# Attention with a mixture of experts on one core: the PV group is issued between the score pair and the maximum passes instead of behind both

## The chip, the core and the metric

The kernel runs on one core of a Trainium2 chip. The number is device time in microseconds for one launch, the median of several runs. The engines here: TensorE (PE in the rows; its weight loads are listed apart, as PEld), VectorE (DVE), ScalarE (ACT), GpSimd (POOL) and SyncE (SP), which issues most transfers. Each runs its own instruction stream in order, and semaphores hold an instruction until others have finished.

## What is computed

One layer: cross attention with residual, then a feed-forward block with residual. B = 8, C = 256 channels, T = 512; 16 heads of 16 channels, attention over the 512 columns of the context.

```python
# attention: x is _layernorm(x), c is ctx_2048
q = jnp.einsum('oc,bct->bot', Wq, x) + bq[None, :, None]   # k, v alike from c
scores = jnp.einsum('bhkt,bhks->bhts', q, k) * SCALE
p = jax.nn.softmax(scores, axis=-1)
out = jnp.einsum('bhts,bhks->bhkt', p, v)
# ... output projection Wo, added to x
# feed-forward: router, softmax, top 2 of 8 experts, and a shared expert
moe = jnp.einsum('te,ted->td', w_dense, eo)
sh = jax.nn.silu(ht @ sw_gate) * (ht @ sw_up) @ sw_down
x = x + moe + sh
```

## The kernel before

The kernel has two stages. The attention stage comes first; the feed-forward stage (shared expert, routing, then 39 blocks of gathered rows) follows it. The change is in the attention stage alone.

The attention works through 16 halves (`HALVES`), each of 8 heads of one batch element; `s` numbers them. A half has 32 units (`UNITS`): one unit is a 128 x 512 tile of scores of one head. Two jobs run beside each other on TensorE:

- `scores(s, u)` (L646 to L660, matmul at L658) multiplies keys by queries, with the row maxima already folded into two extra rows of the operands, and ACT then takes the exponential of the tile (L555) into `probs`. It writes one of three banks of `st_ps` and waits until the exponential of three units before has emptied it.
- `max_pass(n, u)` (L616 to L627, matmul at L625) computes the same scores the other way round for a later half (one to two halves ahead), only so that DVE can take the row maxima (L751, `negmax`). It writes one of three banks of `smax_ps` and waits until the maximum of three passes before is taken (`pe.wait_ge(max_done, i - MAXBUF + 1)`).

`pv(k)` (L662 to L675, matmuls at L671) multiplies the probabilities of four units by the values. It needs the exponentials of all four (`pe.wait_ge(exp_done, GH * (k + 1))`), and is issued in the step after them. `project_qk`, `project_v`, `project_out` and `turn_max` are larger or single products for later or earlier halves: query and key projection (L597, u = 2 and 6, for half s + 3), value projection (L612) in even halves or output projection (L272) in odd halves from 3 on (u = 18 and 26; in half 0 u = 10 and 14), and the transposition of the maxima (L644, u = 12; in half 0 u = 16).

The loop over `u` in steps of two, in the function for TensorE (L704 to L728), is written out by hand and sets the order: two scores, then as many maximum passes as `maxima_until(s, u)` allows (four per pair early in half 0, then three, then two; none behind the last half), then the PV group if `u` is a multiple of 4, then the larger products. The DVE function walks through the same `maxima_until` table (L795 on), and adds behind the maxima: `max_parts` at u = 14, `residual` (L339) at u = 20 and 28 and its statistics (L793) at u = 22 and 30 in odd halves from 3 on, and a few steps of the layer norm in halves 1 to 3 and 14.

Of the kernel before, what the change touches and what calls it, by code (L numbers as in the profile page):

```python
# [21 lines left out]
GH = 4  # L22
UNITS = HH * TT
STEPS = UNITS // GH
# [25 lines left out]
def xattn_ffn_kernel(nc, x, ctxt, wqkv_t, wo_t, bias_cols, rms_w, router_t, gate_up, down,  # L50
# [16 lines left out]
    with ExitStack() as outer:  # L67
# [116 lines left out]
        def turn_unit(s):  # L184

            return 16 if s == 0 else 12

        def late_units(s):

            return (10, 14) if s == 0 else (18, 26)  # L190

        def value_batch(s):

            return s // 2 + 1 if s % 2 == 0 and s // 2 + 1 < B else None

        def maxima_until(s, u):

            pairs = u // TILES + 1
            if s == 0:
                ahead = min(UNITS + AHEAD + 4 * pairs, UNITS + AHEAD + 4 + 3 * pairs, UNITS + AHEAD + 12 + 2 * pairs)  # L200
            elif s < 3:
                ahead = min(80 + 36 * (s - 1) + 3 * pairs, 84 + 36 * (s - 1) + 2 * pairs)
            else:
                ahead = UNITS * (s + 2) - 8 + 2 * pairs
            return min(ahead, UNITS * HALVES)
# [19 lines left out]
        def out_batch(s):  # L225

            return (s - 3) // 2 if s % 2 == 1 and s >= 3 else None
# [4 lines left out]
        def score_bank(i):  # L232
            return st_ps[:, i % STBUF, :]
# [122 lines left out]
        with nc.Block() as block:  # L356
# [211 lines left out]
            def _(pe):  # L568
# [11 lines left out]
                def project_qk(n, i):  # L580
                    s = n - 3
                    if i == 0:
                        pe.wait_ge(c_loaded[(n // 2) % 2], 16 * (n // 4 + 1))
                        if n == 1:
                            pe.wait_ge(qk32_ready, 2)
                        if n == 2:
                            pe.wait_ge(vt_copied, 2)
                        if s >= 0:
                            pe.wait_ge(nm_parts_ready, turns(s))
                            pe.wait_ge(vt_copied, values_before(s))  # L590
                            pe.wait_ge(x1_ready, X1_START + CT * outputs_before(s))
                    else:
                        pe.wait_ge(qk32_ready, 2 * n + 1)
                        pe.wait_ge(xn_ready, n // 2 + 1)
                    src = c_sb[:, (n // 2) % 2, :, :] if i == 0 else xn
                    for kt in range(CT):
                        mm = nc.tensor.matmul(proj_ps[:, :], w_t[:, i, kt, (n % 2) * P:(n % 2) * P + P],  # L597
                                              src[:, kt, :], start=(kt == 0), stop=(kt == CT - 1))
                    mm.then_inc(qk_ready, 1)

                def project_v(b, r):

                    if r == 1:
                        pe.wait_ge(vt_copied, 2 * b + 1)
                    elif b < 2:
                        pe.wait_ge(qk32_ready, 4 * (b + 1))
                    else:
                        pe.wait_ge(nm_parts_ready, turns(2 * b - 1))
                    for i in range(2):
                        st = 2 * r + i  # L610
                        for kt in range(CT):
                            mm = nc.tensor.matmul(proj_ps[:, C * i:C * (i + 1)], c_sb[:, b % 2, kt, st * P:(st + 1) * P],  # L612
                                                  w_t[:, 2, kt, :], start=(kt == 0), stop=(kt == CT - 1))
                    mm.then_inc(v_ready, 1)

                def max_pass(n, u):  # L616
                    buf = n % NBUF
                    if u == 0:
                        pe.wait_ge(stack_loaded[buf], 16 * 2 * 2 * TILES * (n // NBUF + 1))
                    i = UNITS * n + u  # L620
                    if i >= MAXBUF:
                        pe.wait_ge(max_done, i - MAXBUF + 1)
                    tile, pair, tt = u % TILES, u // TILES // TT, u // TILES % TT
                    low = HALFP * tile
                    nc.tensor.matmul(smax_bank(i), q_stack[buf][low:low + SROWS, pair, tt * P:(tt + 1) * P],  # L625
                                     k_stack[buf][low:low + SROWS, pair, :], start=True, stop=True,
                                     tile_position=(low, 0)).then_inc(s_ready, 1)  # L627
# [11 lines left out]
                def turn_max(n):  # L639
                    pe.wait_ge(qk32_ready, 2 * min(n + 3, HALVES))  # L640
                    pe.wait_ge(vt_copied, values_before(max(n - 1, 1)))
                    pe.wait_ge(x1_ready, X1_START + CT * outputs_before(n - 1))
                    pe.wait_ge(max_done, UNITS * (n + 1))
                    nc.tensor.transpose(proj_ps[0:UNITS, 0:P], negmax[:, n % 2, :], ident[:, :]).then_inc(nm_turned, 1)  # L644

                def scores(s, u):  # L646
                    g, st, j = u // (GH * TT), u // GH % TT, u % GH
                    buf = s % NBUF
                    if s == 0 and u == 0:
                        pe.wait_ge(first_loaded, 16 * TILES)  # L650
                        pe.wait_ge(ones_loaded, 16 * TILES * NBUF)
                    if u == (HALF_UNITS if s == 0 else 0):
                        pe.wait_ge(rows_loaded[buf], 16 * TILES * (s // NBUF + 1))
                    i = UNITS * s + u
                    if i >= STBUF:
                        pe.wait_ge(exp_done, i - STBUF + 1)
                    low, pair, end = HALFP * (j % TILES), 2 * g + j // TILES, HALFP * (j % TILES) + SROWS + PARTS
                    nc.tensor.matmul(score_bank(i), k_stack[buf][low:end, pair, st * P:(st + 1) * P],  # L658
                                     q_stack[buf][low:end, pair, :], start=True, stop=True,
                                     tile_position=(low, 0)).then_inc(st_ready, 1)  # L660

                def pv(k):  # L662
                    n, g, st = k // STEPS, k // TT % 2, k % TT
                    pe.wait_ge(exp_done, GH * (k + 1))
                    if st == 0 and k >= TT:
                        pe.wait_ge(pv_copied, k // TT)
                    if st == 0 and g == 0:
                        pe.wait_ge(vt_copied, 2 * (n // 2 + 1))
                        pe.wait_ge(v_ones, min(n + 1, NBUF))
                    for j in range(GH):  # L670
                        mm = nc.tensor.matmul(pv_ps[32 * j:32 * j + 32, :], v_t[n % NBUF][:, st, GH * g + j, :],  # L671
                                              probs[:, k % 2, j, :], start=(st == 0), stop=(st == TT - 1),
                                              tile_position=(0, 32 * j))
                    mm.then_inc(pv_done, 1)
# [29 lines left out]
                for s in range(HALVES):  # L704
                    for u in range(0, UNITS, TILES):
                        scores(s, u)
                        scores(s, u + 1)
                        while passed < maxima_until(s, u):
                            max_pass(passed // UNITS, passed % UNITS)
                            passed += 1  # L710
                        if u % GH == 0 and STEPS * s + u // GH >= 1:
                            pv(STEPS * s + u // GH - 1)
                        if s + 3 < HALVES and u in KQ_UNITS:
                            project_qk(s + 3, KQ_UNITS.index(u))
                        if u == turn_unit(s) and s + 1 < HALVES:
                            turn_max(s + 1)
                        if value_batch(s) is not None and u in late_units(s):
                            project_v(value_batch(s), late_units(s).index(u))
                        if out_batch(s) is not None and u in late_units(s):
                            for kt in range(CT):  # L720
                                project_out(pe, out_batch(s), late_units(s).index(u), kt, proj_ps[:, :])
                        if s == HALVES - 2 and u == 12:
                            pe.wait_ge(max_done, UNITS * HALVES)
                        if UNITS * s + u > UNITS * (HALVES - 2) + 12 and u % GH == 2:
                            filler(smax_bank(0))
# [691 lines left out]
```

## Time and profile before

| what | value |
|---|---|
| median of 3 runs | 936.95 us (926.53 to 937.61) |
| the profiled execution | 931.33 us |
| its span (first to last instruction) | 929.5 us |
| PE busy | 863.4 us, 93% |
| DVE busy | 484.5 us, 52% |
| ACT busy | 400.0 us, 43% |
| maxima (L751 on DVE) | 512, 323.6 us |
| exponentials (L555 on ACT) | 512, 279.3 us |
| PV matmul rows (L671) | 1024 (8 for each of 128 groups), 138.9 us |
| score matmuls (L658), maximum passes (L625) | 512 each, 157.2 and 142.0 us |

Rows of the trace give the start of an instruction, or of a run of equal ones, in microseconds from the span's start, and how long it was busy. Matmuls are pipelined, so a start is a better mark than an end: two matmuls on different rows of the array overlap, and a row of two lasts hardly longer than one. A weight load (PEld) shows the wait of the matmul that it belongs to.

### The profile page before, as it was taken

Reading aid. Unit: us, or ns where it says so; the run is one execution under the profiler, and the core shown is the slowest. Engines: PE = TensorE matmul, PEld = TensorE weight load, DVE = VectorE, ACT = ScalarE, POOL = GpSimd, SP = SyncE. Lnnn points to the kernel's source line nnn. Section 1 sums busy time; section 2 is a strip of 40 time slices with the busy share of each in tenths; the row PEclk is TensorE's granted clock in tenths of the full one; section 3 lists DMA queues with packets and bytes.
Section 4 is the critical chain, followed back from the end, with each engine's and each line's share of the span. In section 5 each row is a group of like instructions: output and inputs, shape, how many; then the busy total and the mean of one; then the engine's idle time right before and its main releaser. Section 6 shows DMA issues by size and latency. Waiting matters only on the chain. (4 is left out here: it accounts for less than half of the span.)

```text
span 929.5 us, 10794 instructions
## 1 busy us (share of the span) xinstructions
PE 863.4 (93%) x3575; PEld 373.2 (40%) x3575; DVE 484.5 (52%) x978; ACT 400.0 (43%) x755; POOL 223.5 (24%) x206
## 2 busy tenths in 40 slices
PE   6699989999999999999999989969999999999992
PEld 2234334334333343333432345725444444444440
DVE  4486788777777777777786056491221111111110
ACT  1104666656666676676765741300012222222220
POOL 3113013213142131421100021000104444444441
PEclk9798999999999999999997989799999999999997
DMA  6877465645655566555611139400725555555542
GB/s 221 183 181 180 95 153 129 150 96 130 146 133 116 114 145 144 135 110 105 140 40 39 37 92 369 164 1 2 278 82 91 91 91 90 91 91 91 91 80 34
DMA packets 46872, 110.43 MB, mean 119 GB/s; under 512 B 11668, under 2 KB 12692, under 8 KB 42580
## 3 DMA queue, kind: packets, MB, share of 16 engines
q1 hardware_dynamic: 35404, 80.23, 34.6%
q0 software_dynamic: 11328, 29.37, 15.6%
q8 instruction: 30, 0.49, 0.2%
q14 instruction: 22, 0.18, 0.1%
q10 hardware_dynamic: 88, 0.16, 0.0%
HBM read 68.44 MB, written 41.16 MB: 118 GB/s over the span
## 5 line engine op out<-in xcount | busy, mean ns | idle before, releaser
L751 DVE TENSOR_REDUCE negmax<-smax_ps 128x1 f32<-128x512 f32 x512 | 323.6, 682 | 107.7 <-PE smax_ps L625 107.5
L555 ACT ACTIVATE probs<-st_ps 128x512 f32<-128x512 f32 x512 | 279.3, 600 | 188.4 <-PE st_ps L658 188.1
L658 PE MATMUL st_ps<-q_stack,k_stack 50*128 50x512 f32 x512 | 157.2, 495 | 10.6 <-ACT probs L555 8.2
L625 PE MATMUL smax_ps<-k_stack,q_stack 48*128 48x512 f32 x512 | 142.0, 438 | 13.5 <-DMA q_stack<-parts_dram 6.9
L1178 PE MATMUL big_ps<-w_gu,attn 128*128 x312 | 140.4, 593 | 0.8 <-ACT attn L1019 0.8
L671 PE MATMUL pv_ps<-probs,v_t 128*32 128x512 f32 x1024 | 138.9, 615 | 0.8 <-ACT probs L555 0.5
L658 PEld LDWEIGHTS st_ps<-q_stack,k_stack 50*128 50x128 f32 x512 | 60.1, 186 | 185.7 <-ACT probs L555 148.7
L985 POOL DMA_INDIRECT out<-x_sb,row_i x39 | 61.7, 1582 | 140.0 <-ACT x_sb L1026 130.2
L1364 DVE TENSOR_TENSOR zeros<-attn,big_ps 128x256 f32<-128x256 f32 x39 | 16.4, 422 | 135.0 <-ACT attn L1038 135.0
L625 PEld LDWEIGHTS smax_ps<-k_stack,q_stack 48*128 48x128 f32 x512 | 67.5, 188 | 46.5 <-DVE negmax L751 29.2
L1178 PEld LDWEIGHTS big_ps<-w_gu,attn 128*128 128x128 f32 x312 | 56.2, 190 | 57.0 <-issue 57.0
L1146 PE MATMUL big_ps<-rows_or_down,zeros 128*128 x156 | 73.5, 593 | 0.6 <-DVE zeros L1356 0.6
L334 POOL TENSOR_TENSOR attn<-attn,recip 128x512 f32<-128x512 f32 x15 | 19.2, 1280 | 223.7 <-DMA recip<-rec_dram 223.7
L1038 ACT ACTIVATE attn<-big_ps 128x256 f32<-128x256 f32 x39 | 15.0, 385 | 117.7 <-PE big_ps L1178 117.7
L1072 PE MATMUL big_ps<-ht_all,sh_gu 128*128 128x512 f32 x128 | 60.8, 632 | 0.7 <-DVE pv_raw L1205 0.7
L970 POOL DMA_INDIRECT x_sb<-h_rows,row_i x39 | 38.8, 995 | 91.9 <-DMA out<-x_sb 80.3
L458 POOL CAST parts<-qk 128x512 fp32r<-128x512 f32 x28 | 17.1, 612 | 173.7 <-ACT qk L508 171.0
L1356 DVE COPY zeros<-big_ps 128x256 f32<-128x256 f32 x39 | 16.6, 425 | 58.5 <-PE big_ps L1155 58.5
L1026 ACT ACTIVATE x_sb<-big_ps,weight 128x512 f32<-128x512 f32 x39 | 26.8, 687 | 45.0 <-PE big_ps L1146 34.9
L462 POOL TENSOR_TENSOR parts<-qk,parts 128x512 fp32r<-128x512 f32 x32 | 40.7, 1273 | 21.5 <-DVE parts L743 19.3
L1072 PEld LDWEIGHTS big_ps<-ht_all,sh_gu 128*128 128x128 f32 x128 | 25.7, 204 | 32.5 <-issue 32.5
L597 PE MATMUL proj_ps<-c_sb,w_t 128*128 128x512 f32 x64 | 36.7, 701 | 1.2 <-ACT qk L508 0.9
(156 smaller groups left out, 719.0 us busy)
## 6 DMA issues: line engine op xcount, KB each, us to landing
parts_dram<-parts SPq DMA_DIRECT2D x32, 512.0 KB, 6.1
k_stack<-parts_dram SPq DMA_DIRECT2D x32, 256.0 KB, 4.9
q_stack<-parts_dram SPq DMA_DIRECT2D x32, 256.0 KB, 5.6
w_gu<-in_gate_up SPq DMA_DIRECT2D x8, 1024.0 KB, 15.5
x_sb<-in_x SPq DMA_DIRECT2D x8, 512.0 KB, 8.1
c_sb<-in_ctx POOLq DMA_DIRECT2D x8, 512.0 KB, 7.9
k_stack<-parts_dram SPq DMA_DIRECT2D x32, 128.0 KB, 5.4
q_stack<-parts_dram SPq DMA_DIRECT2D x32, 128.0 KB, 6.1
```

What stands on the lines that cost most here:

```text
L462: nc.gpsimd.tensor_tensor(parts[:, i, 1, :], qk32[:, i, :], parts[:, i, 0, :].bitcast(F32), ALU.subtract).then_inc(low_ready, 1)
L555: nc.scalar.activation(probs[:, k % 2, u % GH, :], score_bank(UNITS * s + u), ACT.Exp, scale=SCALE).then_inc(exp_done, 1)
L597: mm = nc.tensor.matmul(proj_ps[:, :], w_t[:, i, kt, (n % 2) * P:(n % 2) * P + P], src[:, kt, :], start=(kt == 0), stop=(kt == CT - 1))
L625: nc.tensor.matmul(smax_bank(i), q_stack[buf][low:low + SROWS, pair, tt * P:(tt + 1) * P], k_stack[buf][low:low + SROWS, pair, :], start=T ...
L658: nc.tensor.matmul(score_bank(i), k_stack[buf][low:end, pair, st * P:(st + 1) * P], q_stack[buf][low:end, pair, :], start=True, stop=True, ...
L671: mm = nc.tensor.matmul(pv_ps[32 * j:32 * j + 32, :], v_t[n % NBUF][:, st, GH * g + j, :], probs[:, k % 2, j, :], start=(st == 0), stop=(s ...
L751: nc.vector.tensor_reduce(negmax[:, n % 2, c:c + 1], smax_bank(UNITS * n + u), AX_X, ALU.max, negate=True).then_inc(max_done, 1)
L970: nc.gpsimd.indirect_dma_start(h_in[:, k % RING, :], None, h_rows, bass.IndirectOffsetOnAxis(ap=row_i[:, k:k + 1], axis=0)).then_inc(in_lo ...
L985: nc.gpsimd.indirect_dma_start(out_rows, bass.IndirectOffsetOnAxis(ap=row_i[:, k:k + 1], axis=0), y_sb[:, k % RING, :], None, compute_op=A ...
L1072: mm = nc.tensor.matmul(big_ps[:, 2 * (j % 2) + i, :], sh_gu[:, a, i * F + c * P:i * F + (c + 1) * P], ht_all[:, g, a, :], start=(a == 0), ...
L1146: mm = nc.tensor.matmul(y_ps[:, k % 2, :], act_t[:, a, :], w_dn[:, bass.ds(expert, 1), a, :], start=(a == 0), stop=(a == FT - 1))
L1178: mm = nc.tensor.matmul(gu_ps[:, :], h_t[:, k % 2, a, :], w_gu[:, bass.ds(expert, 1), a, :], start=(a == 0), stop=(a == DT - 1))
```

## The change

The call of `pv` moves up by four lines: in the half-steps with `u` a multiple of 4 the PV group is now issued right behind the two scores and ahead of the maximum passes. Its waits and its operands are the same. No instruction is added or removed, and the order on DVE, ACT, POOL and SP is the same as before.

```diff
--- before.py
+++ after.py
@@ -705,11 +705,11 @@
                     for u in range(0, UNITS, TILES):
                         scores(s, u)
                         scores(s, u + 1)
+                        if u % GH == 0 and STEPS * s + u // GH >= 1:
+                            pv(STEPS * s + u // GH - 1)
                         while passed < maxima_until(s, u):
                             max_pass(passed // UNITS, passed % UNITS)
                             passed += 1
-                        if u % GH == 0 and STEPS * s + u // GH >= 1:
-                            pv(STEPS * s + u // GH - 1)
                         if s + 3 < HALVES and u in KQ_UNITS:
                             project_qk(s + 3, KQ_UNITS.index(u))
                         if u == turn_unit(s) and s + 1 < HALVES:
```

On TensorE, at the start of half 3 (u = 0 to 8), before. `st_ps` rows are score pairs, `smax_ps` rows maximum passes, `pv_ps` rows the PV group, `proj_ps` rows the key and query projections:

```order
L658 MATMUL st_ps<-q_stack3,k_stack3 128x512 x2
L625 MATMUL smax_ps<-k_stack0,q_stack0 128x512 x2
L671 MATMUL pv_ps<-probs,v_t2 32x512 x4
L658 MATMUL st_ps<-q_stack3,k_stack3 128x512 x2
L625 MATMUL smax_ps<-k_stack0,q_stack0 128x512 x2
L597 MATMUL proj_ps<-c_sb,w_t 128x512 x2
L658 MATMUL st_ps<-q_stack3,k_stack3 128x512 x2
L625 MATMUL smax_ps<-k_stack0,q_stack0 128x512 x2
L671 MATMUL pv_ps<-probs,v_t3 32x512 x4
L658 MATMUL st_ps<-q_stack3,k_stack3 128x512 x2
L625 MATMUL smax_ps<-k_stack0,q_stack0 128x512 x2
L597 MATMUL proj_ps<-xn,w_t 128x512 x2
L658 MATMUL st_ps<-q_stack3,k_stack3 128x512 x2
```

The same place in the changed kernel:

```order
L658 MATMUL st_ps<-q_stack3,k_stack3 128x512 x2
L671 MATMUL pv_ps<-probs,v_t2 32x512 x4
L625 MATMUL smax_ps<-k_stack0,q_stack0 128x512 x2
L658 MATMUL st_ps<-q_stack3,k_stack3 128x512 x2
L625 MATMUL smax_ps<-k_stack0,q_stack0 128x512 x2
L597 MATMUL proj_ps<-c_sb,w_t 128x512 x2
L658 MATMUL st_ps<-q_stack3,k_stack3 128x512 x2
L671 MATMUL pv_ps<-probs,v_t3 32x512 x4
L625 MATMUL smax_ps<-k_stack0,q_stack0 128x512 x2
L658 MATMUL st_ps<-q_stack3,k_stack3 128x512 x2
L625 MATMUL smax_ps<-k_stack0,q_stack0 128x512 x2
L597 MATMUL proj_ps<-xn,w_t 128x512 x2
L658 MATMUL st_ps<-q_stack3,k_stack3 128x512 x2
```

In each step the PV row has changed places with the passes in front of it. The passes of u = 0 (and 4) now stand one score pair ahead of the passes of u = 2 (and 6), with nothing else between; and between the passes of u = 2 and those of u = 4 there are the projection, the scores and the PV group.

On TensorE at the start of half 1, where three passes follow a pair, before and then changed:

```order
L658 MATMUL st_ps<-q_stack1,k_stack1 128x512 x2
L625 MATMUL smax_ps<-k_stack2,q_stack2 128x512 x3
L671 MATMUL pv_ps<-probs,v_t0 32x512 x4
L658 MATMUL st_ps<-q_stack1,k_stack1 128x512 x2
L625 MATMUL smax_ps<-k_stack2,q_stack2 128x512 x3
L597 MATMUL proj_ps<-c_sb,w_t 128x512 x2
L658 MATMUL st_ps<-q_stack1,k_stack1 128x512 x2
L625 MATMUL smax_ps<-k_stack2,q_stack2 128x512 x3
```

```order
L658 MATMUL st_ps<-q_stack1,k_stack1 128x512 x2
L671 MATMUL pv_ps<-probs,v_t0 32x512 x4
L625 MATMUL smax_ps<-k_stack2,q_stack2 128x512 x3
L658 MATMUL st_ps<-q_stack1,k_stack1 128x512 x2
L625 MATMUL smax_ps<-k_stack2,q_stack2 128x512 x3
L597 MATMUL proj_ps<-c_sb,w_t 128x512 x2
L658 MATMUL st_ps<-q_stack1,k_stack1 128x512 x2
L671 MATMUL pv_ps<-probs,v_t1 32x512 x4
```

Here six passes stand with only one score pair in the middle. In the last half, and in half 14 from u = 8 on, there are no passes, and the order is the same in both kernels.

## Rows read from the trace of the kernel before

**Rows 1.** Page, part 1: busy us (share of the span) x instructions.

```profile
PE 863.4 (93%) x3575; PEld 373.2 (40%) x3575; DVE 484.5 (52%) x978; ACT 400.0 (43%) x755; POOL 223.5 (24%) x206
```

**Rows 2.** Timeline of PE, half 4, u = 20 to 28: start, us, what.

```profile
217.21 0.50 PE L658 MATMUL st_ps<-q_stack,k_stack 50*128 50x512 f32 x2
217.55 0.40 PE L625 MATMUL smax_ps<-k_stack,q_stack 48*128 48x512 f32 x2
217.87 1.07 PE L671 MATMUL pv_ps<-probs,v_t 128*32 128x512 f32 x8
218.87 0.51 PE L658 MATMUL st_ps<-q_stack,k_stack 50*128 50x512 f32 x2
219.20 0.41 PE L625 MATMUL smax_ps<-k_stack,q_stack 48*128 48x512 f32 x2
219.44 1.10 PE L658 MATMUL st_ps<-q_stack,k_stack 50*128 50x512 f32 x2
220.05 0.82 PE L625 MATMUL smax_ps<-k_stack,q_stack 48*128 48x512 f32 x2
220.81 1.06 PE L671 MATMUL pv_ps<-probs,v_t 128*32 128x512 f32 x8
...
222.14 0.39 PE L625 MATMUL smax_ps<-k_stack,q_stack 48*128 48x512 f32 x2
222.46 1.99 PE L612 MATMUL proj_ps<-w_t,c_sb 128*128 128x256 f32 x8
224.38 0.50 PE L658 MATMUL st_ps<-q_stack,k_stack 50*128 50x512 f32 x2
```

**Rows 3.** Timeline of DVE, half 4, behind u = 26 and 30.

```profile
222.56 1.29 DVE L751 TENSOR_REDUCE negmax<-smax_ps 128x1 f32<-128x512 f32 x2 [0.44 <-PE smax_ps L625]
...
226.82 0.69 DVE L751 TENSOR_REDUCE negmax<-smax_ps 128x1 f32<-128x512 f32 x1 [0.38 <-PE smax_ps L625]
```

**Rows 4.** Timeline of all engines, half 7, around u = 24.

```profile
306.75 0.74 DVE L339 SCALAR_TENSOR_TENSOR x_sb<-proj_ps,bo_all,x_sb 128x512 f32<-128x512 f32 x1
...
307.41 1.28 DVE L751 TENSOR_REDUCE negmax<-smax_ps 128x1 f32<-128x512 f32 x2
...
307.62 0.50 PE L658 MATMUL st_ps<-q_stack,k_stack 50*128 50x512 f32 x1 [0.22 <-ACT probs L555]
...
308.14 0.18 PEld L625 LDWEIGHTS smax_ps<-k_stack,q_stack 48*128 48x128 f32 x1 [0.34 <-DVE negmax L751]
...
308.57 1.06 PE L671 MATMUL pv_ps<-probs,v_t 128*32 128x512 f32 x8
308.60 0.68 DVE L793 BATCH_NORM_STATS2 stats<-x_sb 128x6 f32<-128x512 f32 x1
309.20 2.46 DVE L751 TENSOR_REDUCE negmax<-smax_ps 128x1 f32<-128x512 f32 x4
...
312.27 0.50 PE L658 MATMUL st_ps<-q_stack,k_stack 50*128 50x512 f32 x2
```

**Rows 5.** Waits, 197.3 to 461.1 us: us in total, times, longest.

```profile
PEld smax_ps L625 <- DVE negmax L751: 4.4, 18, 0.3
```

**Rows 6.** Timeline of PE, half 15, u = 8.

```profile
524.73 0.50 PE L658 MATMUL st_ps<-q_stack,k_stack 50*128 50x512 f32 x2
525.16 1.06 PE L671 MATMUL pv_ps<-probs,v_t 128*32 128x512 f32 x8
```

**Rows 7.** Timeline of ACT, half 4, u = 26 and 27.

```profile
222.33 1.08 ACT L555 ACTIVATE probs<-st_ps 128x512 f32<-128x512 f32 x2 [0.87 <-PE st_ps L658]
```

**Rows 8.** Timeline of PE, half 2, u = 4 and 8.

```profile
141.19 0.50 PE L658 MATMUL st_ps<-q_stack,k_stack 50*128 50x512 f32 x2
...
146.25 0.50 PE L658 MATMUL st_ps<-q_stack,k_stack 50*128 50x512 f32 x2
```

**Rows 9.** Windows: busy us of PE, PEld, DVE, ACT, POOL; PEclk, DMA share, GB/s.

```profile
197.30:461.10 263.80, 257.92 (x1348) 99.25 (x1345) 197.18 (x333) 177.34 (x345) 64.44 (x57) 1.00 0.58 128
493.90:507.60 13.70, 13.44 (x45) 3.68 (x41) 8.24 (x39) 5.95 (x12) 0.00 (x0) 0.50 0.20 41
```

## Prediction, made before the changed kernel was timed

> **What bounds the kernel now.** I read the page's busy shares first, then the stage by windows, then the timeline of TensorE (PE) with that of VectorE (DVE) and ScalarE (ACT) beside it, and last the waits. PE is busy for 93% of the span [rows 1]. The change touches only the attention stage (66.8 to about 547 us); what follows it keeps its order.
>
> I call the work of a step, which is four units (u, u+1, u+2, u+3 with u a multiple of 4): **S** a pair of score matmuls (L658), **P** the group of PV matmuls (L671), **J** a projection (L597, L612 or L272, about 1.9 us), **F** the pair of maximum passes (L625) of the half-step that has P, **R** the pair of the half-step without P. Before, PE runs S F P S R (J), now S P F S R (J). The J's stand only behind an R.
>
> In the timeline of an ordinary stretch [rows 2] one step without J reads: S 217.21, F 217.55, P 217.87, S 218.87, R 219.20, next S 219.44. That last pair's row lasts 1.10 us where others last 0.50: its second score waits until 220.05, where the passes start with it, and P follows at 220.81. The delay before 220.05 is the exponential: a score matmul goes to one of three PSUM banks, and its bank must have been emptied. From S (218.87) to that second score (220.05) are 1.18 us. Let me call this the **ACT latency**. The maximum passes have three banks too, so the second pass of a pair waits for the maximum of the first pass of the pair before it. From a pass to its maximum: pass 222.14, maximum starts 222.56; two last 1.29 us and one 0.69, so the first ends 1.10 us behind its pass and the next 0.60 later [rows 2, 3]. The release costs 0.05 us (a maximum from 307.41 ends at 308.09, the weight load behind it starts at 308.14) [rows 4]. So the **DVE latency** is 1.15 us.
>
> Before, this latency is almost free. Between F and R stands P, 1.0 us; between R and the next F stands either J, 1.9 us, or the ACT latency, which covers the DVE latency exactly (passes at 219.20 and 220.05). In the nine halves from 197.3 to 461.1 the passes' weight loads waited for DVE 4.4 us in all [rows 5].
>
> **The change, part by part.** No instruction is added or removed, and no other engine's order moves. What moves is P, over F. Three terms follow.
>
> *1. P comes earlier.* It now stands right behind S. Where no passes are left (the last half) it stands so already: S 524.73, P 525.16, so S to P is 0.43 us against 0.33 for S to the passes (218.87 to 219.20) [rows 2, 6]. P needs the exponential of unit u-1, which ends one ACT interval behind the one that released the second score: two take 1.08 us, so about 0.50 [rows 7]. Thus P starts 0.43 us behind an unstalled S, or 0.50 behind a stalled second score, instead of 0.66 (217.21 to 217.87) or 0.76 (220.05 to 220.81). F follows P by 1.00 us, taken from P to S (217.87 to 218.87). The next S follows F by 0.24 (219.20 to 219.44) to 0.32 (222.14 to 222.46, a pair to J); I take 0.27. So the middle S lies at 1.70 us, where it lay at 1.66. Nothing is gained by P's earlier start, since F is only moved behind it.
>
> *2. R loses its distance to F.* Between F and R stands only one S pair. The first pass of R would start at 1.70 + 0.33 = 2.03 us and is free; the second waits for the first maximum of F, at 1.43 + 1.15 = 2.58 us. That is a stall of 0.55 us in every step. Behind it in PE's order are the next S, or J. What it costs depends on that.
>
> Step without J: the next second score needs 1.70 + 1.18 = 2.88 us by the ACT latency anyway; the stall gives 2.58 + 0.33 (second pass to second score, as 219.20 behind 218.87) = 2.91. Before: 217.21 to 220.05, 2.84. **Loss 0.07 us**; the cover is the ACT latency. In the step that turns the maxima (u = 12) a transpose stands between P or F and S, the ACT latency then ends last by more, and I put its loss at 0.
>
> Step with J: J cannot start before the stalled pass. A stalled single pass to the next full-array group is 0.43 us (308.14 to 308.57), and J to S 1.92 (222.46 to 224.38) [rows 2, 4]. From an unstalled S: 2.58 + 0.43 + 1.92 = 4.93. Before: 0.66 + 1.00 + 0.33 + 0.32 + 1.92 = 4.23. **Loss 0.70**. From a stalled second score: 0.50 + 1.00 + 1.15 + 0.43 + 1.92 = 5.00 against 220.05 to 224.38, 4.33. **Loss 0.67.** Nothing gives it back: the ACT latency counts from an S that is itself late.
>
> A half of s = 3 to 12 has J in four of its eight steps (u = 2, 6, 18, 26): 3 x 0.67 + 0.70 + 3 x 0.07 = 2.9 us. Ten such halves: **29.0 us**.
>
> The Trainium skill (TensorE: Matmul & The Clock Gate, Step-by-step: what each phase is for) says that weight loads are pulled ahead of running matmuls while matmuls keep program order; by that, J could start 0.33 rather than 0.43 behind the stalled pass, and the sum would fall by some 4 us. The measured 0.43 decides, being the same case of a pass that waits for DVE.
>
> *3. Where DVE has more to do.* In odd halves from 3 on, DVE also adds the residual behind F and takes statistics behind R, 0.66 us (306.75 to 307.41) and 0.60 us (308.60 to 309.20) of its time [rows 4]. With F now 1 us later they fall together: from S of the step, F's maxima end at 2.53 and 3.13, residual 3.79, R's 4.39 and 4.99, statistics 5.59, next F's first maximum 6.19. That F starts at 2.91 + 1.50 = 4.41, so its maximum is 0.68 late, and the R before J with it. Before, the same place has a stall too: 307.62 to 312.27 is 4.65 against 4.33 [rows 2, 4]. Net 0.68 - 0.32 = 0.36 us, twice for each of five halves: **3.6 us**.
>
> In s = 0 to 2 the pairs are three passes for some steps. The third R pass then waits for F's third maximum, 1.43 + 1.10 + 1.20 + 0.05 = 3.78; J at 4.21, next S 6.13, against 141.19 to 146.25, 5.06 [rows 8]. **Loss 1.07**, in two such steps each of s = 0, 1, 2: 6.4 us. The four-pass steps of s = 0 run at DVE's pace in both orders (0). The two later J's of s = 2 bring 1.3, the rest of s = 1 and 2 some 0.5, while two steps of s = 1 with extra statistics on DVE may win 0.4 each: **7.4 us** in all. Half 13 and the first steps of 14 have two J's, 0.36 twice and small losses: **2.4 us**. From u = 8 of half 14 no pass is left and nothing changes.
>
> Sum: 29.0 + 3.6 + 7.4 + 2.4 = 42.4 us. The profiled execution took 931.3 us (span 929.5), 5.6 below the median of the runs, inside their spread. 931.3 + 42.4 = **974 us**.
>
> **Bounds.** F to S at 0.24 or 0.32 only moves the stall's start, not its end. If the second pass of F could overlap the end of P, the release comes up to 0.1 earlier: 44 J steps x 0.1 = 4.4 less. If the residual's backlog costs nothing new, 4 less; if the losses with ACT's cover are 0.15 instead of 0.07, 5 more. With the runs' own spread (5 us down, 6 up): 958 to 988 for this case.
>
> **Rivals.** *The stall is absorbed.* PE's waits are short, so a stall might be only an existing wait moved. For it: steps without J do just that. Against: the four steps with J of each half have no wait between F and the end of J. Time if it holds everywhere: 128 x 0.07 = 9, some 940 us. Chance 0.07.
>
> *Faster.* P takes the place of a wait in front of the DVE-bound passes: the present stall in the odd halves (0.32 us, 12 times) and 0.8 in s = 1 vanish: 931.3 - 3.8 - 0.8 = 926.7 us. It decides only if R's second pass were released within about 0.1 us of its natural start, which 1.15 against 0.61 us excludes as far as these rows show. Chance 0.03.
>
> *The clock falls.* With PE stalled more often the chip may grant less. From 493.9 to 507.6 the clock stood at 0.50, which is 1.2 GHz [rows 9]. At that clock TensorE's work takes up to twice as long, its waits no longer; I take a third of the stretch as lost. Three further stretches of 13.7 us give 974 + 3 x 4.6 = 988. Against it: the clock is 1.00 (2.4 GHz) from 197.3 to 461.1, with waits of 0.6 us such as the one before 220.05 all through it [rows 2, 9]. Chance 0.08.
>
> **How the numbers follow.** Forecast 0.82. The range takes part of the smaller losses and the clock case: 955 to 990. About 2% (19 us) is what a measurement can tell from no change. Only "absorbed" and a little of the forecast's low tail lie within: same 0.09, faster 0.03, slower 0.88.
>
> **What would show it.** In the profile after, the wait of L625's weight loads on DVE, 4.4 us now, should be about 0.5 us in nearly every step, over 30 us in the same nine halves; steps with J should be 4.9 to 5.0 us (from the score that starts last) instead of 4.2 to 4.3, steps without J hardly longer; the part behind the attention unchanged. If the second pass of R starts right behind its S, the DVE latency is wrong; if steps without J grow by as much as the others, the cover by ACT is.

## The result

| kernel | median | runs | profiled execution | span |
|---|---|---|---|---|
| before | 933.0 us | 926.5 to 937.6 | 931.3 us | 929.5 us |
| changed | 974.1 us | 969.9 to 980.5 | 976.5 us | 974.7 us |

The ratio is 1.048, with a 95% interval of 1.042 to 1.054: the changed kernel is 41 us slower. The forecast was 974 us. The runs of one kernel can lie in a faster group and in a slower one with a lower mean granted clock, and every ratio here is taken over the faster group.

The same place as in [rows 2], half 4, u = 20 to 28, in the timeline of PE in the changed kernel (start, us busy, what):

```profile
238.64 0.50 PE L658 MATMUL st_ps<-q_stack,k_stack 50*128 50x512 f32 x2
239.08 1.06 PE L671 MATMUL pv_ps<-probs,v_t 128*32 128x512 f32 x8
240.07 0.50 PE L625 MATMUL smax_ps<-k_stack,q_stack 48*128 48x512 f32 x2
240.41 0.40 PE L658 MATMUL st_ps<-q_stack,k_stack 50*128 50x512 f32 x2
240.65 0.40 PE L625 MATMUL smax_ps<-k_stack,q_stack 48*128 48x512 f32 x1
241.35 0.49 PE L625 MATMUL smax_ps<-k_stack,q_stack 48*128 48x512 f32 x1 [0.31 <-DVE negmax L751]
241.35 0.72 PE L658 MATMUL st_ps<-q_stack,k_stack 50*128 50x512 f32 x2
242.00 1.06 PE L671 MATMUL pv_ps<-probs,v_t 128*32 128x512 f32 x8
243.00 0.50 PE L625 MATMUL smax_ps<-k_stack,q_stack 48*128 48x512 f32 x2
243.33 0.39 PE L658 MATMUL st_ps<-q_stack,k_stack 50*128 50x512 f32 x2
243.57 0.39 PE L625 MATMUL smax_ps<-k_stack,q_stack 48*128 48x512 f32 x1
244.28 0.49 PE L625 MATMUL smax_ps<-k_stack,q_stack 48*128 48x512 f32 x1 [0.32 <-DVE negmax L751]
244.70 1.99 PE L612 MATMUL proj_ps<-w_t,c_sb 128*128 128x256 f32 x8
246.62 0.51 PE L658 MATMUL st_ps<-q_stack,k_stack 50*128 50x512 f32 x2
```

S is at 238.64, P at 239.08, F at 240.07, the middle S at 240.41. The first pass of R starts at 240.65, in its natural place; the second starts at 241.35, and its row names the maximum on DVE as what it waited for. The next S stands behind it. One step later the same happens at 244.28, and here the projection stands behind: 244.70, and the next S only at 246.62. From the second score of u = 24 (241.35 + 0.33) to that S it is 4.94 us; in [rows 2] it was 4.33 (220.05 to 224.38).

DVE beside it:

```profile
243.53 2.48 DVE L751 TENSOR_REDUCE negmax<-smax_ps 128x1 f32<-128x512 f32 x4 [0.45 <-PE smax_ps L625]
```

F's pass starts at 243.00. Its first maximum starts at 243.53 and lasts about 0.68 us (the row holds four of them), so it ends at about 244.21, and the second pass of R starts 0.07 us later. The waits in the changed kernel from 197.3 to 461.1, the same times as in [rows 5]:

```profile
PEld smax_ps L625 <- DVE negmax L751: 69.7, 97, 1.1
...
PE smax_ps L625 <- DVE negmax L751: 20.6, 55, 0.7
...
PEld st_ps L658 <- ACT probs L555: 2.9, 8, 0.4
```

And in the kernel before, between the same times:

```profile
PE st_ps L658 <- ACT probs L555: 3.9, 18, 0.2
PEld st_ps L658 <- ACT probs L555: 85.8, 126, 0.8
```

The passes' weight loads waited 69.7 us for DVE, against 4.4 before. That sum overstates it: a weight load counts as waiting while the matmuls in front of it still run. The pass matmuls themselves were held 20.6 us, 55 times (none before); the start of the next score pair, not this sum, tells the price. ACT held the score matmuls 18 times before and does not hold them once now, and their loads hardly wait for it (2.9 us against 85.8, a sum that overstates in the same way): the wait for the exponential has been replaced by one for the maximum.

The place of [rows 4], half 7 at u = 24, PE and then DVE:

```profile
341.34 0.70 PE L625 MATMUL smax_ps<-k_stack,q_stack 48*128 48x512 f32 x2
...
342.15 0.49 PE L625 MATMUL smax_ps<-k_stack,q_stack 48*128 48x512 f32 x1
343.34 0.50 PE L625 MATMUL smax_ps<-k_stack,q_stack 48*128 48x512 f32 x1 [0.70 <-DVE negmax L751]
343.76 1.98 PE L272 MATMUL proj_ps<-attn,w_o 128*128 128x512 f32 x4
```

```profile
340.15 0.74 DVE L339 SCALAR_TENSOR_TENSOR x_sb<-proj_ps,bo_all,x_sb 128x512 f32<-128x512 f32 x1
...
342.01 0.68 DVE L793 BATCH_NORM_STATS2 stats<-x_sb 128x6 f32<-128x512 f32 x1
342.61 2.46 DVE L751 TENSOR_REDUCE negmax<-smax_ps 128x1 f32<-128x512 f32 x4
```

The residual and the statistics push the first maximum of F (pass at 341.34) back to 342.61, and the second pass of R starts at 343.34. That is 1.19 us behind the first pass of R (342.15).

Two things in the windows do not belong to this pattern. The first three columns are the busy times of PE, PEld and DVE, and the number behind POOL's is the granted clock. The changed kernel, half 14 (542.8 to 567.6), half 1 up to u = 8, and half 2 up to u = 8:

```profile
542.80:567.60 24.80, 23.30 (x116) 7.11 (x116) 14.71 (x61) 18.44 (x35) 1.28 (x1) 1.00 0.16 38
107.60:124.90 17.30, 16.26 (x57) 5.34 (x57) 9.02 (x15) 6.82 (x14) 1.88 (x2) 0.80 0.43 103
142.80:163.00 20.20, 19.67 (x60) 6.78 (x60) 9.15 (x16) 7.35 (x14) 2.16 (x3) 0.66 0.36 89
```

The kernel before, half 14 and halves 1 and 2:

```profile
487.90:518.70 30.80, 29.02 (x119) 8.22 (x116) 14.21 (x60) 18.82 (x36) 1.28 (x1) 0.78 0.13 30
105.40:166.10 60.70, 56.80 (x300) 22.22 (x297) 51.20 (x86) 39.12 (x77) 15.20 (x15) 1.00 0.56 132
```

In the changed kernel the clock fell to 1.2 GHz in halves 1 and 2, where it was full before, and it stayed full in half 14, where it fell before. Half 14 became 5.5 us shorter.

Step by step, from the second score of each step in the two traces, the attention stage lost 50.3 us (50.4 from the first score to the last exponential):

| part | forecast | measured |
|---|---|---|
| halves 0 to 2 | 7.4 | 18.0 |
| halves 3 to 12 | 32.6 | 35.5 |
| half 13 | 2.4 | 2.4 |
| half 14 | in the row above | -5.5 |
| attention | 42.4 | 50.3 |

The forecast for half 13 includes the start of half 14. The stretch ahead of the first score was 1.4 us shorter, and all that follows the last exponential took 380.0 us against 383.8, so the span grew by 45.2 us.

### The profile page after: what moved, and what is told of

The parts are those of the page before. It is cut to its first block and busy times, and to the rows that moved or that the text cites. A ratio compares the mean times of both kernels' runs of the same rounds, so it can differ in the third digit from the quotient of the medians.

```text
span 974.7 us, 10794 instructions
## 1 busy us (share of the span) xinstructions
PE 887.7 (91%) x3575; PEld 380.5 (39%) x3575; DVE 481.9 (49%) x978; ACT 404.4 (41%) x755; POOL 223.2 (23%) x206
## 5 line engine op out<-in xcount | busy, mean ns | idle before, releaser
L751 DVE TENSOR_REDUCE negmax<-smax_ps 128x1 f32<-128x512 f32 x512 | 318.9, 682 | 165.0 <-PE smax_ps L625 164.9
L555 ACT ACTIVATE probs<-st_ps 128x512 f32<-128x512 f32 x512 | 283.9, 598 | 234.2 <-PE st_ps L658 233.1
L625 PE MATMUL smax_ps<-k_stack,q_stack 48*128 48x512 f32 x512 | 183.3, 484 | 45.6 <-DVE negmax L751 35.7
L625 PEld LDWEIGHTS smax_ps<-k_stack,q_stack 48*128 48x128 f32 x512 | 74.1, 186 | 218.0 <-DVE negmax L751 146.3
L658 PE MATMUL st_ps<-q_stack,k_stack 50*128 50x512 f32 x512 | 141.0, 450 | 1.1 <-ACT probs L555 0.5
L462 POOL TENSOR_TENSOR parts<-qk,parts 128x512 fp32r<-128x512 f32 x32 | 40.7, 1273 | 20.8 <-DVE parts L743 18.5
```

What stands on the lines that cost most here:

```text
L462: nc.gpsimd.tensor_tensor(parts[:, i, 1, :], qk32[:, i, :], parts[:, i, 0, :].bitcast(F32), ALU.subtract).then_inc(low_ready, 1)
L555: nc.scalar.activation(probs[:, k % 2, u % GH, :], score_bank(UNITS * s + u), ACT.Exp, scale=SCALE).then_inc(exp_done, 1)
L751: nc.vector.tensor_reduce(negmax[:, n % 2, c:c + 1], smax_bank(UNITS * n + u), AX_X, ALU.max, negate=True).then_inc(max_done, 1)
```

## The experiments

The theory is the one of the forecast: the second pass of a pair waits for the first maximum of the pair before it (1.15 us by the forecast), and P's new place puts F and R too close; J stands behind the wait. The main rival is that P in front of the passes costs by itself. In the table, "attention" is the time from the first score to the last exponential, and "rest" what follows it, each in one profile. The ratio is to the kernel before on the same chip.

| run | ratio (95%) | attention | rest |
|---|---|---|---|
| before | 1 | 478.9 | 383.8 |
| changed | 1.048 (1.042 to 1.054) | 529.3 | 380.0 |
| short_new | 0.986 (0.977 to 0.995) | 471.4 | 387.6 |
| short_old | 0.963 (0.955 to 0.971) | 458.3 | 379.1 |
| j_steps | 1.036 (1.025 to 1.047) | 524.8 | 390.2 |
| other_steps | 1.036 (1.026 to 1.047) | 522.0 | 379.7 |
| j_first | 0.996 (0.993 to 1.000) | 478.7 | 389.3 |
| halves_0_2 | 1.023 (1.013 to 1.032) | 500.4 | 387.3 |
| from_half3 | 1.043 (1.035 to 1.051) | 511.5 | 390.2 |
| half14 | 0.989 (0.981 to 0.997) | 472.9 | 379.4 |
| other_short | 0.984 (0.976 to 0.992) | 463.3 | 387.0 |
| late_scale | 0.989 (0.984 to 0.993) | 479.2 | 387.2 |
| late_scale_half14 | 0.988 (0.983 to 0.992) | 472.5 | 378.9 |
| mixed | 0.997 (0.994 to 1.001) | 476.7 | 379.3 |

"Rest" is the same code in all of them and takes from 378.9 to 390.2 us. It goes with the time at 1.2 GHz in it, the last 12 to 14 us left out, which ran at that clock in every profile: 20 to 24 us where it took 379 to 380, 31 in the kernel before with its 383.8, and 37 to 44 where it took 387 to 390. For the attention the profiles are therefore the better witness than the medians.

### The maximum made short

```diff
-    nc.vector.tensor_reduce(negmax[:, n % 2, c:c + 1], smax_bank(UNITS * n + u),
+    nc.vector.tensor_reduce(negmax[:, n % 2, c:c + 1], smax_bank(UNITS * n + u)[:, 0:32],
```

in the changed kernel (short_new) and in the one before (short_old). The results are then shifted by a wrong maximum; the work on PE is the same.

> The changed order, but each maximum is taken over the first 32 of its 512 columns only (so the softmax is shifted by a wrong maximum). Theory (the second pass of a pair waits for the first maximum of the pair before it): the maximum takes some 0.2 us instead of 0.68, the stall shrinks from 0.93 to about 0.4 us behind the natural place or less, and the gap between the two orders nearly closes: within 10 us of the old order with the same short maxima, some 925 to 940 us. Rival (P in front of the passes costs by itself: its wait for the exponential, or the change between the two kinds of matmul): the gap to the old order with short maxima stays near 41 us.

> The old order with the same short maxima (over 32 of 512 columns). Both theories: PE bounds the ordinary halves, so little is won there; the steps of the first three halves with three and four passes, which run at DVE's pace, get shorter. 915 to 932 us. It is the reference for the short maxima in the changed order.

The gap between the two orders fell from 4.8 to 2.3 points (0.986 against 0.963), about 21 us, where 10 us or less were expected. short_old itself was faster than the 915 to 932 us expected, with a median of 903.0 us: short maxima also took 0.7 us from each half from 4 to 12 of the old order. "Rest" and the clock in halves 0 to 2 are in that number. In the profiles of halves 3 to 13 alone the gap was 37.9 us with full maxima and 18.0 with short ones, so about half of it goes with the length of the maximum. In short_new the step with J looks so, PE and then DVE:

```profile
209.94 0.50 PE L625 MATMUL smax_ps<-k_stack,q_stack 48*128 48x512 f32 x2
210.27 0.40 PE L658 MATMUL st_ps<-q_stack,k_stack 50*128 50x512 f32 x2
210.52 0.69 PE L625 MATMUL smax_ps<-k_stack,q_stack 48*128 48x512 f32 x2
211.14 2.00 PE L612 MATMUL proj_ps<-w_t,c_sb 128*128 128x256 f32 x8
```

```profile
210.47 0.29 DVE L751 TENSOR_REDUCE negmax<-smax_ps 128x1 f32<-128x32 f32 x2 [1.93 <-PE smax_ps L625]
210.95 0.49 DVE L751 TENSOR_REDUCE negmax<-smax_ps 128x1 f32<-128x32 f32 x2 [0.19 <-PE smax_ps L625]
```

The row of R now lasts 0.69 us where an unstalled pair lasts 0.39: its second pass still waits, but 0.2 us instead of 0.7. That is because the maximum still starts 0.53 us behind the pass (209.94 to 210.47), however short it is. Half 4 took 29.3 us before and 33.0 in the changed kernel; with short maxima it took 30.2 in the new and 28.6 in the old order. So the gap of a half went from 3.7 to 1.7 us. In a step with J that starts unstalled the loss went from 0.8 to 0.3, of which 0.2 is the rest of the stall; what is left lies in the distances between the groups.

### Half of the steps each

```diff
+    early = has_product(s, u + 2)
+    if early and u % GH == 0 and STEPS * s + u // GH >= 1:
+        pv(STEPS * s + u // GH - 1)
     while passed < maxima_until(s, u):
...
-    if u % GH == 0 and STEPS * s + u // GH >= 1:
+    if not early and u % GH == 0 and STEPS * s + u // GH >= 1:
         pv(STEPS * s + u // GH - 1)
```

This is j_steps, against the kernel before; `has_product` is true where a projection follows the passes of that u. In other_steps the condition is `not has_product(s, u + 2)`.

> P moved only in the steps whose second half-step has a projection. Theory: these carry nearly all of the loss: an ordinary half lost 2.7 of its 3.3 us there in the trace (plus 0.4 per half by the residual), so about 933 + 36 = 969 us. Rival (the loss is a cost of P's new place in every step): half of the steps, half of the loss, about 953 us.

> P moved only in the steps without a projection. Theory: the wait for the exponential covers the stall, 0.2 us or less in each of 60 steps, and half 14 becomes shorter: 933 to 940 us. Rival (a cost in every step): about 953 us.

Steps with J: each half from 4 to 12 lost 2.7 us, as expected from the trace, and the rest of the 3.7 is what the other steps add. The 1.036 is 33 us, near the 36 expected. The profile lost more in the attention stage, 45.9 us, but it has a stretch at 1.2 GHz from 129.4 to 153.3 in it, which falls into halves 1 and 2, and a longer one than before in half 14.

The other steps cost as much, which refutes the expectation for them, and the losses of the two runs add up to more than that of the changed kernel. Two causes stand in the profile. Halves without a fall of the clock lost 2.4 us, not 0.8: a late R now delays the F of the next step, which in the old order comes right behind its S. And seven times between halves 2 and 13 the clock fell. Half 5 at u = 24:

```profile
258.16 0.72 PE L658 MATMUL st_ps<-q_stack,k_stack 50*128 50x512 f32 x2
258.75 0.50 PE L625 MATMUL smax_ps<-k_stack,q_stack 48*128 48x512 f32 x1
260.01 0.64 PE L625 MATMUL smax_ps<-k_stack,q_stack 48*128 48x512 f32 x1 [0.76 <-DVE negmax L758]
260.58 1.94 PE L671 MATMUL pv_ps<-probs,v_t 128*32 128x512 f32 x8
262.44 0.79 PE L658 MATMUL st_ps<-q_stack,k_stack 50*128 50x512 f32 x2
...
263.59 3.68 PE L272 MATMUL proj_ps<-attn,w_o 128*128 128x512 f32 x4
267.20 0.50 PE L658 MATMUL st_ps<-q_stack,k_stack 50*128 50x512 f32 x2
```

```profile
260.20:267.00 6.80, 6.80 (x17) 1.87 (x16) 3.43 (x6) 1.08 (x2) 1.27 (x1) 0.50 0.74 153
```

The second pass of F waits from 258.75 to 260.01; P then takes 1.86 us to the next S instead of 1.00, and J 3.61 instead of 1.92. Of halves 4 to 12, those with such a stretch lost 5.4 to 5.5 us, so one fall costs 3.0 us, and seven of them some 21 us of the 43 that the attention stage lost. Six of the seven are at u = 24 of an odd half or u = 0 of the next, where DVE has the residual and the statistics. There PE stood idle for 0.75 to 0.76 us as the clock fell. But of eleven such idle stretches in halves 3 to 13 only six have a fall with them.

### The same without the long stalls

other_short is other_steps with the short maxima.

> P moved in the steps without a projection only, with maxima over the first 32 of 512 columns. The same move with full maxima was 3.6% slower than before, and in its profile the clock fell seven times between half 2 and 13, six of them where DVE was behind with the residual and PE stood waiting for it. Theory (the long stalls on DVE bring the clock down, and it is the clock that costs): with short maxima no stall is left, the clock stays full from half 1 to 13, and the time is within 10 us of the old order with short maxima, 903 to 915 us. Rival (the clock falls for another reason, such as the rhythm of the steps): still five or more stretches at 0.5, and 925 us or more.

From 129 to 480 us, halves 2 to 13:

```profile
129.00:480.00 351.00, 343.33 (x1820) 131.93 (x1821) 89.66 (x498) 238.87 (x464) 83.36 (x74) 1.00 0.57 125
```

The clock stayed full, and a half took 28.8 to 28.9 us against 28.6 in short_old. The ratio is 2 points above that of short_old (0.984 against 0.963), more than the 10 us expected. The profile has a fall in halves 0 and 1 (87.9 to 108.4), but so has the one of short_old (96.8 to 107.0), and a "rest" of 387 against 379. So from half 2 on the falls of the clock in this kernel go with the long waits for DVE, though not each wait brings one. Why they come in other_steps and not in the changed kernel is not settled: its waits at the same places are nearly as long (1.19 us from pass to pass against 1.26, with PE idle for 0.70 us against 0.76).

### The projection ahead of the passes

```diff
     scores(s, u)
     scores(s, u + 1)
     if u % GH == 0 and STEPS * s + u // GH >= 1:
         pv(STEPS * s + u // GH - 1)
+    if s + 3 < HALVES and u in KQ_UNITS:
+        project_qk(s + 3, KQ_UNITS.index(u))
...
     while passed < maxima_until(s, u):
         max_pass(passed // UNITS, passed % UNITS)
         passed += 1
-    if s + 3 < HALVES and u in KQ_UNITS:
-        project_qk(s + 3, KQ_UNITS.index(u))
...
```

`project_v` and `project_out` move in the same way; `turn_max` stays behind the passes.

> The changed order, but where a half-step has a projection it is issued ahead of the passes: S P F, then S J R. Theory (R's second pass waits for F's first maximum, and J stands behind that wait): J now runs while DVE takes the maxima, the wait of 0.6 to 0.9 us in the steps with J goes, and what is left is 0.1 to 0.2 us a step: 5 to 15 us above the kernel before. Rival (P's place behind S costs by itself): 30 us or more above it.

Half 4 at u = 24 in the timeline of PE:

```profile
225.05 0.50 PE L625 MATMUL smax_ps<-k_stack,q_stack 48*128 48x512 f32 x2
225.39 0.40 PE L658 MATMUL st_ps<-q_stack,k_stack 50*128 50x512 f32 x2
225.72 1.99 PE L612 MATMUL proj_ps<-w_t,c_sb 128*128 128x256 f32 x8
227.64 0.51 PE L625 MATMUL smax_ps<-k_stack,q_stack 48*128 48x512 f32 x2
227.99 0.40 PE L658 MATMUL st_ps<-q_stack,k_stack 50*128 50x512 f32 x2
```

F at 225.05, S at 225.39, J at 225.72, R at 227.64 with nothing left to wait for, and the next S at 227.99. P stands where the change put it, and the whole loss is gone: halves 4 to 12 took 29.3 us each, as before. The steps with J are now up to 0.2 us shorter than before and those without up to 0.1 longer. P's place costs next to nothing by itself; J behind the stalled pass is what costs. The expectation had left 5 to 15 us, and the ratio of 0.996 lies below it: it holds the 5.5 us won in half 14, and against them 6.1 us lost in halves 0 and 1, with a fall of the clock from 95.6 to 116.1. J ahead of the passes in the old order was not run; the passes' loads waited only 4.4 us there in nine halves [rows 5], so it had little to win.

### By halves

```diff
-    early = has_product(s, u + 2)
+    early = s < 3
```

against j_steps, for halves_0_2; `s >= 3` in from_half3 and `s == 14` in half14.

> P moved in halves 0 to 2 only, where pairs of three and four passes stand. The trace of the changed kernel has 18.0 us of its 50 us of attention loss there, 8 to 10 of them in steps at a granted clock of 0.5. Theory (long stalls of PE there, and the clock falls with them): 12 to 20 us above the kernel before, with stretches at 0.5 between 105 and 165 us. Rival (only the wait for the maxima counts, the clock fell there by chance): 7 to 9 us above it.

> P moved from half 3 on only. By the trace of the changed kernel, halves 3 to 13 lose 37.9 us (3.7 each) and half 14 wins 5.5: 25 to 35 us above the kernel before, with the clock full from half 1 to 13. With the run that moves P in halves 0 to 2 alone the two should add up to the whole, 41 us.

The window from half 0 to half 2 of halves_0_2, and the one from half 1 to half 13 of from_half3:

```profile
67.00:185.00 118.00, 108.96 (x462) 41.53 (x460) 78.22 (x133) 59.79 (x115) 24.66 (x22) 0.88 0.50 120
```

```profile
105.00:495.00 390.00, 359.97 (x1785) 138.90 (x1785) 269.55 (x477) 237.09 (x455) 85.78 (x77) 1.00 0.52 117
```

halves_0_2 lost 18.5 us in these three halves (18.0 in the changed kernel), with the clock at 1.2 GHz in five stretches between 78 and 161 us, where the theory expected such stretches; the ratio puts it 21 us above before, just over the 12 to 20 expected. But long stalls, the theory's reason, are not there before every fall: in the 8 us ahead of each of those in halves 1 and 2 PE stood idle for at most 0.4 us at a time. So what brings the clock down in these halves is open. from_half3 reproduced each half from 4 to 12 of the changed kernel within 0.1 us, won the same 5.5 us in half 14, and had no fall from half 1 to 13. But its ratio puts it 40 us above before, where 25 to 35 were expected, and the medians of the two (21 and 40 us above before, by their ratios) add up to 61 and not to 41. In the attention stage the two profiles add up: 21.5 and 32.6 us, together 54.1, against 50.4 of the changed kernel; the difference is what falls of the clock cost halves_0_2 in half 3 (2.1) and in half 14 (1.3 more than before). In the profiles the larger part of what is left comes from "rest", which was 387.3 and 390.2 us in these, 380.0 in the changed kernel and 383.8 before; for the other runs it was not measured.

The clock in the halves with three-pass pairs is not settled: between half 0's u = 8 and half 3 it fell in the profiles of the changed kernel, j_steps, halves_0_2 and j_first, and not in those of the kernel before, from_half3, half14 and late_scale_half14. It also fell in late_scale (124 to 145 us), mixed (71 to 88 us) and short_old, which have the old order there, and it did not fall in short_new, which has the new one. In short_old the fall, at 96.8, lies in an idle stretch of PE of 4.7 us that begins at 94.3. So the order makes the falls there more frequent at most.

### Half 14

> P moved in half 14 only. In the profiles the half took 30.15 us before, 13.7 of them at a granted clock of 0.5 behind a stall of PE at u = 4, and 24.6 after, at the full clock. Theory (P no longer waits behind the stalled passes, PE works through the stretch and keeps its clock): 3 to 7 us below the kernel before. Rival (that the clock fell there in one profile and not in the other is chance): no difference.

```profile
486.70:511.40 24.70, 23.06 (x119) 6.90 (x116) 14.18 (x60) 18.87 (x36) 1.28 (x1) 1.00 0.17 38
```

The half took 24.1 us instead of 30.1 and kept its clock; the ratio is 0.989. To tell the order from the cause of the stall I moved instead the small DVE operations in the old order:

```diff
-    if s == HALVES - 2 and u in (0, 6, 12):
+    if s == HALVES - 2 and u in (16, 20, 24):
...
-        row_scale(dve, 0, EARLY, (u // 6,))
+        row_scale(dve, 0, EARLY, ((u - 16) // 4,))
```

> The old order, with the three groups of small DVE operations of half 14 (the row statistics for the next stage) moved from u = 0, 6 and 12 to u = 16, 20 and 24, where no maxima are left. Theory (half 14 is long because its passes wait behind those operations, and the clock falls with that): the half is near 24 us as in the changed order instead of 30, 5 to 8 us below the kernel before. Rival (P's place is what helps there): no gain, 30 us for the half.

> Both: P moved in half 14, and the small DVE operations later. Theory of the stall: they win the same time, so together hardly more than one of them, 6 to 9 us below before. If they are separate gains: 12 us or more below.

Half 14 of late_scale lies within this window of the old order:

```profile
489.00:518.00 29.00, 27.58 (x145) 8.35 (x141) 17.04 (x62) 21.73 (x42) 1.27 (x1) 1.00 0.13 32
```

It took 24.0 us, and the ratio is 0.989 again; both edits together give 24.0 us and 0.988. The three ratios are 10 to 12 us below before, more than expected for each (3 to 7, 5 to 8, 6 to 9), where the attention stage of half14 and late_scale_half14 won 6.0 and 6.4. That of late_scale won nothing, because the fall of the clock in its halves 1 and 2 cost 7.0 us. The two edits win the same time. In the kernel before, a pass issued in half 14 waited for a maximum that stood behind DVE's row statistics:

```profile
491.65 0.49 PE L625 MATMUL smax_ps<-k_stack,q_stack 48*128 48x512 f32 x1
493.04 0.50 PE L625 MATMUL smax_ps<-k_stack,q_stack 48*128 48x512 f32 x1 [0.89 <-DVE negmax L751]
```

```profile
491.29 0.90 DVE L291 BATCH_NORM_AGGREGATE mv<-stats 128x2 f32<-128x6 f32 x12
```

PE stood idle for 0.89 us, and the clock fell for 13.7 us [rows 9]. With either edit the clock did not fall. Most of the 6 us is the clock: from the second score of u = 8 to that of u = 20, where no pass is left in either order, it took 13.3 us before and 8.6 in half14, which is 4.7 of them. The other 1.3 us lie in u = 0 to 7, where the wait and the clock come together.

### A version that might beat both

mixed has the old order in halves 0 to 2, P behind the scores and J ahead of the passes from half 3 on, and the later DVE operations.

> A version that might beat both: the old order in halves 0 to 2, from half 3 on P behind the scores and the projection ahead of the passes, and the small DVE operations of half 14 later. From the profiles: 0.8 us won in half 3, nothing in 4 to 13, 6 in half 14: 6 to 12 us below the kernel before.

The attention stage took 476.7 us with a fall of the clock from 71.1 to 88.2 that cost it 4.1 us in half 0. The ratio of 0.997 (0.994 to 1.001) is no better than the kernel before and misses the 6 to 12 us expected, though half 14 took 24.2 us in the profile; where it is lost in the other runs is open. half14, late_scale and late_scale_half14 are 1.1 to 1.2% faster than the kernel before, and can't be told from one another. Halves 4 to 13 gain nothing from any order tried; half 3 gains 0.6 to 0.8 us with J first.

## Why the prediction was right, step by step

**P comes earlier.** Right in its kind, a little small. S to P is 0.44 (238.64 to 239.08), 0.43 in [rows 6]; P to F 1.00. But F to the middle S is 0.34, not 0.27: I had taken the distance between passes and scores from pairs that follow a score pair, and behind P it is longer. So the middle S lies at 1.77 and not at 1.70. Behind the second score of a stalled step P starts after 0.31 us (241.69 to 242.00), where the forecast had 0.50: in the new order DVE holds the scores back and no longer ACT, and the exponential that P needs is done soon behind them.

**The DVE latency.** The mechanism was right, the term too small. From F to the release of R's second pass it was 1.28 us (243.00 to 244.28), not 1.15: the maximum starts 0.53 us behind a pass that follows P, and 0.42 behind one that follows S [rows 2, 3]; the pass itself lasts 0.50 there and 0.39 here. That makes the stall behind the first pass 0.70 us (240.65 to 241.35).

**Steps with J.** The forecast was 0.70 from an unstalled S and 0.67 otherwise; measured were 0.8, and 0.6 to 0.7. In the second kind two errors nearly cancel: the latency 0.13 us too short, P 0.19 too late. The 0.43 us from the stalled pass to J was read from a PV group (308.57 in [rows 4]), and not from a product over the full array as the text has it; to J it was 0.42. The run j_first shows that J's place behind this wait is the loss.

**Steps without J.** Forecast 0.07, measured 0.2, and 0 at u = 12 as forecast. The cover by ACT holds, but it is 0.13 us too short, because the DVE latency is that much longer. The score loads' waits for ACT are gone (2.9 us).

**The residual in odd halves.** Forecast 0.36 twice for each odd half, measured 0.38 twice: at u = 24 of the odd half and at u = 0 of the next one (0.61 without it against 0.99). So each half from 4 to 12 has one of them, and all lost the same 3.7 us.

**Halves 0 to 2.** This term was the worst: 7.4 against 18.0. Some 8 us of it are falls of the clock in halves 1 and 2, which the forecast had as a rival with 0.08 and at 14 us: four three-pass steps lost 13.0 us together there, where such steps at the full clock in the other profiles lost 1.1 to 1.5 each (forecast 1.07).

**Half 14.** The forecast had a small loss, and it won 5.5 us. I had read the fall of the clock there [rows 9] as a threat and not asked what had caused it, and so not what would take it away.

The last two errors have opposite signs: 10.6 us too little in halves 0 to 2 and 2.9 in halves 3 to 12, against 5.5 won in half 14 and 5.2 in the front and the rest of the kernel, which the edit does not touch. They nearly cancel: the right total rests in its main part, the 35.5 us of halves 3 to 12, on the right mechanism, and in the rest on luck.

**The rivals.** "Absorbed" is refuted by the changed kernel and "faster" with it; that P's place might help where passes stall is true in half 14 (5.5 us) and at u = 20 of half 1 (0.5 us). The clock's rival came in part, where the forecast did not look. Its argument against that rival, waits of 0.6 us at the full clock all through halves 4 to 12, counts from start to start: PE itself stood idle for about 0.2 us in them (0.22 in [rows 4]), and in the changed kernel for up to 0.70. The rule of the Trainium skill on weight loads (TensorE: Matmul & The Clock Gate, Step-by-step: what each phase is for), that they are pulled ahead of running matmuls, would as the forecast read it have had J 0.33 us behind the stalled pass; it was 0.42 (244.28 to 244.70), as the measured row said.

## What to carry to other kernels

When a group is moved in an in-order stream, ask first which two groups of the same ring of buffers it used to keep apart, and what stands behind the second: a wait that another wait already covers costs little, and the same wait in front of a long dense product costs its whole length. If the distance must go, put the long product between the two users of the ring. And take a latency from a place with the same neighbour: here it was 0.11 us longer behind the PV group than behind the scores.

## What was not expected of the hardware

- Moving P only in the steps without a projection brought the granted clock down to 1.2 GHz seven times in the profile, in halves 2 to 13, at 3.0 us each. DVE held its passes for less time in all than those of the changed kernel (13.5 us against 20.6 from 197.3 to 461.1), where the clock stayed full from half 3 to 13; its longest idle stretches were 0.76 us against 0.70. With short maxima, which take the long waits on DVE away, it did not fall there.
- The feed-forward part, identical in all kernels, took 379 to 390 us in single profiles, with 20 to 44 us of it at 1.2 GHz. That is as large as several of the effects looked for. It may be much of the scatter between runs, but only one execution of each kernel was profiled.
- A maximum over 32 columns still started 0.53 us behind its pass: shortening the operation can't bring the release below that.
